# Raw weight pieces ahead of stores and convolution loads, and a new order in the first group, in a two-layer convolution and FFN kernel

## What is computed

```python
# layer 0
h   = grouped_conv1d(x, weight, taps=9, groups=4) + (c @ c_weight.T)[:, :, None] + bias
y   = h @ W.T + bias_k + lora(h)        # W: 1024 x 1024, low-rank part of rank 3 x 16
x   = x + y
# layer 1
att = softmax(mlp(c))                   # 8 experts' weights per batch
h   = (att-weighted 64 x 64 matrix) @ x + (att @ bias_k)[:, :, None]
s   = h @ Wr.T                          # 64 scores per token, the best 16 kept, softmax -> G
z   = ((h @ A) * G) @ B                 # A: 1024 x 1024, B: 1024 x 1024
x   = x + 2 * z
```

## Time and profile before

| | |
|---|---|
| runs | 703.81, 704.87, 707.1 us: median 704.87 |
| the profiled execution | 702.36 us |
| its span | 700.5 us, at a mean granted clock of 0.975 |
| TensorE (PE) | busy 662.5 us (95%) |
| VectorE (DVE) | busy 452.5 us (65%) |
| ScalarE (ACT) | busy 213.0 us (30%) |
| GpSimd (POOL) | busy 77.9 us (11%) |
| DMA | 157.98 MB, mean 226 GB/s |

### The profile page before, as it was taken

One profiled execution on the slowest core, in us unless ns is written; L12 is line 12 of the kernel. 1 busy time (PEld: TensorE's weight loads), 2 busy tenths in 40 slices (PEclk: granted clock), 3 DMA queues, 4 the chain that ended last, 5 costly groups with the idle time before them and its releaser, 6 DMA issues.

```text
span 700.5 us, 8826 instructions
## 1 busy us (share of the span) xinstructions
PE 662.5 (95%) x3197; PEld 546.1 (78%) x3197; DVE 452.5 (65%) x688; ACT 213.0 (30%) x275; POOL 77.9 (11%) x91
## 2 busy tenths in 40 slices
PE   9979999949789999999799999999799999999996
PEld 8858888837578788888589888887588978888875
DVE  2877866628248749626957858645866965756764
ACT  2631434215023412323413411323512521243510
POOL 1599200000000024000000006000000000000000
PEclk9998999979989999999999999999999999999999
DMA  8589744773973771076797664066688566127594
GB/s 286 201 283 390 276 194 139 276 265 115 387 245 122 300 300 61 31 271 221 284 338 253 265 257 157 11 231 226 232 302 308 197 263 274 30 97 214 203 334 177
DMA packets 51449, 157.98 MB, mean 226 GB/s; under 512 B 5472, under 2 KB 6368, under 8 KB 51424
## 3 DMA queue, kind: packets, MB, share of 16 engines
q1 hardware_dynamic: 46096, 148.05, 58.2%
q10 hardware_dynamic: 5328, 9.61, 4.2%
HBM read 131.94 MB, written 25.71 MB: 225 GB/s over the span
## 4 chain that ended last, share of the span: by engine, by line
PE 51%; DMA 7%; DVE 5%; issue 3%; ACT 2%; SPq 1%; ACTq 0%; DVEq 0%
PE bank L1304 13%; PE bank L1306 13%; PE bank L1305 13%; PE bank L1318 6%; DMA raw<-pieces 4%; PE bank L1338 3%; PE bank L1325 2%; DMA gate_x<-gates 1%; DMA piece_lo<-kept 1%; ACT piece_hi L603 1%; DVE piece_lo L846 1%; DVE work L941 1%; PE bank L1344 1%; PE bank L1330 1%; PE bank L1332 1%
## 5 line engine op out<-in xcount | busy, mean ns | idle before, releaser
L846 DVE TENSOR_TENSOR piece_lo<-raw,piece_hi 128x1024 fp32r<-128x1024 f32 x60 | 74.2, 1241 | 101.7 <-ACT piece_hi L603 101.7
L1304 PE MATMUL bank<-piece_hi,u_hi 128*128 128x512 f32 x272 | 113.8, 418 | 25.2 <-DVE piece_lo L996 15.4
L603 ACT ACTIVATE piece_hi<-raw 128x1024 fp32r<-128x1024 f32 x60 | 63.1, 1057 | 160.3 <-PE bank L1306 109.4
L1305 PE MATMUL bank<-piece_lo,u_hi 128*128 128x512 f32 x272 | 111.6, 410 | 0.0
L1306 PE MATMUL bank<-piece_hi,u_lo 128*128 128x512 f32 x272 | 111.2, 409 | 0.0
L1304 PE MATMUL bank<-v_hi,piece_hi 128*128 128x512 f32 x256 | 101.9, 398 | 0.0
L1306 PE MATMUL bank<-v_hi,piece_lo 128*128 128x512 f32 x256 | 101.1, 395 | 0.0
L1305 PE MATMUL bank<-v_lo,piece_hi 128*128 128x512 f32 x256 | 100.9, 394 | 0.0
L1304 PEld LDWEIGHTS bank<-piece_hi,u_hi 128*128 128x128 f32 x272 | 54.1, 199 | 41.9 <-DVE piece_lo L996 16.7
L1304 PE MATMUL bank<-piece_hi,v_hi 128*128 128x512 f32 x192 | 75.9, 396 | 0.7 <-DMA piece_lo<-kept 0.7
L1306 PE MATMUL bank<-piece_hi,v_lo 128*128 128x512 f32 x192 | 75.8, 395 | 0.0
(11 more groups left out here) (141 smaller groups left out, 820.8 us busy)
## 6 DMA issues: line engine op xcount, KB each, us to landing
raw<-pieces SPq DMA_DIRECT2D x84, 512.0 KB, 4.9
piece_hi<-kept SPq DMA_DIRECT2D x48, 512.0 KB, 4.6
piece_lo<-kept SPq DMA_DIRECT2D x48, 512.0 KB, 5.6
conv_in<-conv_x SPq DMA_DIRECT2D x16, 516.0 KB, 6.5
x<-x SPq DMA_DIRECT2D x16, 512.0 KB, 5.1
gate_x<-gates ACTq DMA_DIRECT2D x32, 256.0 KB
out<-x SPq DMA_DIRECT2D x32, 256.0 KB, 2.3
conv_in<-pieces SPq DMA_DIRECT2D x12, 512.0 KB, 7.9
```

What stands on the lines that cost most here:

```text
L603: act.activation(piece_hi[:, n % SLOTS, :], raw[:, r % RAWS, :], ACT.Copy).then_inc(s_piece_hi, 1)
L846: dve.tensor_tensor(piece_lo[:, n % SLOTS, :], raw[:, r % RAWS, :], piece_hi[:, n % SLOTS, :].bitcast(F32), ALU.subtract).then_inc(s_piece ...
L1304: pe.matmul(to, left_hi, right_hi, start=first, stop=False)
L1305: pe.matmul(to, left_hi, right_lo, start=False, stop=False)
```

## The change

On SP, in the first group: `next_raw(8)` goes ahead of the loads and stores of sums; the stores of unit 2 are taken apart in pairs, with raw 16 between them and raw 17 behind them, and the loads of unit 3 follow raw 17 in one block; the stores of unit 3 and the convolution loads are taken in pairs with raw 22 and raw 23 between them. In the loop, each of the four convolution loads follows one of `next_raw(16)` to `(19)`, and the two bias tables follow `next_raw(20)` and `next_raw(21)`.

On ScalarE and VectorE, in the first group: the low-rank mask and factors come ahead of split 5, and VectorE's `combine(0)` is cut in two, with mask and factors between its halves; splits 5 and 6 come ahead of the halves of unit 0's sums; on ScalarE split 11 comes ahead of the copy of the scores and split 13 and two halves of unit 2 ahead of the copy of the gates; split 14 comes ahead of the gate loads; `combine(3)` moves from behind the gated chunks to behind chunk 5, and split 19 to behind chunk 7.

```diff
--- before.py
+++ after.py
@@ -406,12 +406,12 @@
                 sp.wait_ge(s_out_ctx, 16)
                 cond_bias(0)
                 next_raw(7)
+                next_raw(8)
                 for i in range(4):
                     sp.wait_ge(s_comb_in[i], 16)
                     load_weights(1, i)
                 for step in range(4):
                     keep_weights(0, step)
-                next_raw(8)
                 next_raw(9)
                 next_raw(10)
                 for step in range(2):
@@ -424,17 +424,26 @@
                 mix_bias(0)
                 next_raw(14)
                 next_raw(15)
+                keep_weights(2, 0)
+                keep_weights(2, 1)
                 next_raw(16)
-                for step in range(4):
-                    load_weights(3, keep_weights(2, step))
-                for n in range(17, 22):
+                keep_weights(2, 2)
+                keep_weights(2, 3)
+                next_raw(17)
+                for i in range(4):
+                    load_weights(3, i)
+                for n in range(18, 22):
                     next_raw(n)
-                for step in range(4):
-                    keep_weights(3, step)
-                for t in range(NT):
-                    load_conv_in(1, t)
+                keep_weights(3, 0)
+                keep_weights(3, 1)
                 next_raw(22)
+                keep_weights(3, 2)
+                keep_weights(3, 3)
+                load_conv_in(1, 0)
+                load_conv_in(1, 1)
                 next_raw(23)
+                load_conv_in(1, 2)
+                load_conv_in(1, 3)
                 next_raw(24)
                 for t in range(NT):
                     store(0, t, 0, t + 1)
@@ -468,17 +477,18 @@
                 next_raw(15)
                 for n in range(11, 14):
                     fetch(g, n)
-                next_raw(16)
-                next_raw(17)
-                next_raw(18)
-                next_raw(19)
+                for n in range(16, 20):
+                    next_raw(n)
+                    if not last:
+                        load_conv_in(g + 1, n - 16)
+                next_raw(20)
                 if not last:
-                    for t in range(NT):
-                        load_conv_in(g + 1, t)
                     cond_bias(g)
+                next_raw(21)
+                if not last:
                     mix_bias(g)
-                for n in range(20, 24):
-                    next_raw(n)
+                next_raw(22)
+                next_raw(23)
                 next_raw(24)
                 next_raw(25)
                 fetch(g, 26)
@@ -732,14 +742,12 @@
                 split_first(3)
                 split_first(4)
                 biases_out(1, s_mixb, 3, s_out_mixb)
-                split_first(5)
-                for step in range(2):
-                    combined_hi(0, step)
                 mix_bias()
                 lora_parts(0)
-                for step in range(2, 4):
+                split_first(5)
+                split_first(6)
+                for step in range(4):
                     combined_hi(0, step)
-                split_first(6)
                 split_first(7)
                 split_first(8)
                 for step in range(4):
@@ -750,25 +758,28 @@
                     if c % 2 == 0:
                         act.wait_ge(s_comb[c // 2], 32 * 2)
                     split_hi(0, MIX0 + c, v_hi[:, c, :], work[:, c, :])
+                split_first(11)
                 score_out(0, 4)
-                split_first(11)
                 gates_exp(0)
                 split_first(12)
+                split_first(13)
+                combined_hi(2, 0)
+                combined_hi(2, 1)
                 gates_out(0, 6)
-                split_first(13)
+                combined_hi(2, 2)
+                combined_hi(2, 3)
+                split_first(14)
                 act.wait_ge(s_gates_out, 16)
                 for c in range(GATES):
                     spread_gates(c)
-                for step in range(4):
-                    combined_hi(2, step)
-                split_first(14)
                 split_first(15)
                 for c in range(NCH):
                     if c % 2 == 0:
                         act.wait_ge(s_comb[c // 2], 32 * 3)
                     gated_hi(0, c)
-                    if c in (1, 3, 5, 6):
+                    if c in (1, 3, 5):
                         split_first(16 + c // 2)
+                split_first(19)
                 for step in range(4):
                     combined_hi(3, step)
                 for n in range(20, 24):
@@ -996,13 +1007,16 @@
                     dve.tensor_tensor(piece_lo[:, n % SLOTS, :], raw[:, n % RAWS, :],
                                       piece_hi[:, n % SLOTS, :].bitcast(F32), ALU.subtract).then_inc(s_piece_lo, 1)
 
-                def combine(unit):
-
-                    for i in range(4):
-                        dve.wait_ge(s_comb_in[i], 16 * (unit + 1))
+                def combine(unit, part=None):
+
                     b11, b12, b21, b22 = (raw_weights(unit, i) for i in range(4))
-                    dve.tensor_tensor(b11, b12, b11, ALU.subtract).then_inc(s_sum, 1)
-                    dve.tensor_tensor(b12, b22, b12, ALU.subtract).then_inc(s_sum, 1)
+                    if part != 1:
+                        for i in range(4):
+                            dve.wait_ge(s_comb_in[i], 16 * (unit + 1))
+                        dve.tensor_tensor(b11, b12, b11, ALU.subtract).then_inc(s_sum, 1)
+                        dve.tensor_tensor(b12, b22, b12, ALU.subtract).then_inc(s_sum, 1)
+                    if part == 0:
+                        return
                     dve.wait_ge(s_sum, 4 * unit + 2)
                     dve.tensor_tensor(b22, b22, b11, ALU.subtract).then_inc(s_sum, 1)
                     dve.wait_ge(s_sum, 4 * unit + 3)
@@ -1047,13 +1061,14 @@
                 mix_bias()
                 dve.wait_ge(s_adapter, 14)
                 split_first(4)
-                combine(0)
-                split_first(5)
+                combine(0, 0)
                 masked(0, 4)
                 lora_rest(0)
+                combine(0, 1)
+                split_first(5)
+                split_first(6)
                 for step in range(4):
                     combined_lo(0, step)
-                split_first(6)
                 split_first(7)
                 for h in range(2):
                     for t in range(NT):
@@ -1087,9 +1102,11 @@
                 split_first(12)
                 split_first(13)
                 combine(2)
-                for step in range(4):
-                    combined_lo(2, step)
+                combined_lo(2, 0)
+                combined_lo(2, 1)
                 split_first(14)
+                combined_lo(2, 2)
+                combined_lo(2, 3)
                 split_first(15)
                 dve.wait_ge(s_lo, H0)
                 for c in range(NCH):
@@ -1097,9 +1114,11 @@
                     if c % 2 == 0:
                         dve.wait_ge(s_comb[c // 2], 32 * 3)
                     gated_lo(0, c)
-                    if c in (1, 3, 5, 6):
+                    if c in (1, 3, 5):
                         split_first(16 + c // 2)
-                combine(3)
+                    if c == 5:
+                        combine(3)
+                split_first(19)
                 for step in range(4):
                     combined_lo(3, step)
                 for n in range(20, 23):
```

## The result

The median after is 685.71 us (682.83 to 686.93 in four runs) against 705.94 in the four runs beside it: a ratio of 0.9715, with an interval of 0.9679 to 0.9751, or 20.2 us less. The forecast was 670.5 with a range of 663 to 684. The direction was right and the size was not: about two fifths of the expected gain are missing, and the time lies 1.7 us beyond the range.

The account below looks back on a forecast made before the run. TensorE was taken as the bound, busy 95% of the span, gains coming from waits and lowered clock. 702.4 - 23.4 (first group) - 11.3 (loop) + 1.0 (opening, mix) = 668.7; 671.2 by the median, stated 670.5, range 663 to 684.

Parts of the forecast that it names:

- The loop: Middle loop groups: convolution loads behind raw loads bring piece 20 earlier; the whole difference from the last group, 11.3 us, won.
- Rival two: Loop: its gain fails because the gate loads were slow, not piece 20; 682 us, chance 0.10.
- The opening and the mix: First group's start: earlier mask wins 5.3 us, not kept; TensorE waits at mix and score 4 instead; 1.0 us lost.
- The reason given for the late last store: Opening: raw 7 and on leave SP 4.6 us later, behind split 5, so unit 1's last store lands at 94.1 to 96.7.
- the 2.3 us of the estimate: Opening: by the skill's exclusion rule a moved VectorE sum could wait out a GpSimd instruction, 2.3 us; not counted.
- The middle of the first group: Three waits for raw pieces' low halves go with their clock loss: 22.0 us, 23.4 with the loop's first convolution.
- margins of 4 to 5 us: Middle of the first group: least time by which pieces, 19 and 20, would be ready before TensorE needs them.
- rival one: Middle: loads come later because stores and loads share engines, overrunning margins; 6 to 8 us more, 678; chance 0.17.
- The loop's first convolution: Its 1.4 us wait for four additions goes, as splits for the next group end near 183, before TensorE's last product.
- Rival three: Opening: its 5.3 us are kept since unit 1's stores don't land later; 665 us, chance 0.09.
- rival four: Middle: unit 3's sums wait for late loads, delaying gate products; slower from a landing at about 183, 709 up; chance 0.02.
- rival five: Whole kernel: nothing moves, other waits of the same size stand behind those named; 703 to 706 us, chance 0.04.

Follow-up runs that it names:

- e6: The changed kernel with split 5 ahead of the low-rank factors on ScalarE and right behind the mask on VectorE: 682.92 us, ratio 0.9714.
- e3: The changed kernel with gate loads turned to 16 ranks outermost instead of eight rows, A and B laid out to match: 678.9 us, ratio 0.9645.
- e5: The changed kernel with VectorE's four additions ahead of its split of the third piece for group 1: 677.1 us, ratio 0.962.
- e2: The changed kernel with the loop's SP order of before: 697.55 us, ratio 0.9914.
- e10: e7 plus raw 23 straight behind raw 22 on SP: 669.04 us, ratio 0.9507.
- e9: The changed kernel with raw 23 straight behind raw 22 on SP, ahead of the last four stores and the convolution loads: 685.46 us, ratio 0.9742.
- e7: The changed kernel with gate loads 16 outermost, unit 3 sums behind split 19, additions ahead of the third split, split 5 early: 669.43 us, ratio 0.9508.

## Why the prediction was right or wrong

**The loop: right.** Both waits for `u_lo` are gone, and with them the 4.3 us for line 846's low halves, which the prediction left out of its list of waits ("nearly all idle time lies in a few places": of 38.0 us idle the list has 25.2) but had in its 11.3 us, as that was taken from the whole stretch. Piece 20 of group 1 is split at 297.76, 15.7 us after the transposed scores (about 15 was named); the middle groups take 79.32 and 78.82 us (79 to 80 were named), and the loop's part alone gives them 10.1 us. Rival two, that the gate loads were at fault and the order wouldn't help, fell. It had half a point: the gate loads do hold half of the engines, and in the kernel of before they were one of two things late.

**The opening and the mix: right in place, partly by luck in size.** The mask runs at 46.92 (46.65 was named) and TensorE resumes at 49.22 (49.45), after 0.95 us at a clock of 1.00. Raw 7 leaves at 52.97 (53.5), the last store of unit 1 is waited for until 95.08 (94.1 to 96.7), and the transposed scores are 1.0 us later (101.97 before, 103.00 after), just the 1.0 that was taken. The new wait came at the mix items in one piece of 4.2 us, with 1.7 of clock, where two of 2 and 3 were named. That TensorE simply comes early is borne out: VectorE's addition that it waits for starts at 85.93, and before at 85.97. The reason given for the late last store isn't. SP issues the first store of unit 1 at 74.67 before, 74.97 after and 74.44 in e6, whether raw 7 left at 48.91, 52.97 or 48.40. So the start of the raw pieces doesn't set it, and that the scores come just 1.0 us later is luck. VectorE's sums of unit 1, which those stores wait for, start at 65.00, 66.08 and 65.12. By the row of before, VectorE's four low halves beside GpSimd were to stay at 1.15 us each. Here the four take 6.57 us, 1.64 each. Three of them in VectorE's timeline:

```profile
54.42 4.89 DVE L1031 TENSOR_TENSOR v_lo<-work,v_hi 128x1024 fp32r<-128x1024 f32 x3
```

That is some 0.5 us more each, beside a GpSimd busy 4.66 of these 4.89 us. So what the Trainium skill (SBUF — State Buffer, section Who interferes with whom) says of the two engines' exclusion bore on this placing where I went by the row, and the row itself had another side. Before, the low halves kept their 1.15 us and GpSimd's two copies beside them lasted 6.29 us (from 51.61); after, with two of VectorE's sums beside them, the copies last 2.63 us (from 49.23). The moved sums take 1.21 and 1.30 us (1.53 and 1.65 before), so nothing near the 2.3 us of the estimate shows there. What the longer low halves cost the kernel wasn't separated.

**The middle of the first group: wrong in the size of the DMA queue.** The step that failed is "the DMA queue served in order at 1.26 us per load or store: [...] about 17 us of work". First, the count was wrong by its own terms: eight stores, two pieces and four loads are 14 x 1.26 = 17.6 us, and the eight gate loads, half the size, are another 5.0, so 22.7. Second, the price was wrong for the gate loads. Alone they move some 190 GB/s on half of the engines (174 to 199 from 121 to 125 us of before), so 256 KB take about 1.38 us of those eight: 17.6 + 8 x 1.38 = 28.7 us, an estimate from these rows, and 29.9 with raw 18 behind them: 148 instead of the 144 named. It landed at 153. The remaining 5 to 6 us stand in the windows at a full share and low rate (318 GB/s from 120 to 130, 353 in e3, when stores and loads are mixed), and their cause wasn't separated. The e3 run takes 4.7 us off piece 18's landing, where the two prices of the gate loads differ by 8 x (1.38 - 0.63) = 6.0.

As a result pieces 17 and 18 were 6 and 9 us later than worked out. The margins of 4 to 5 us were overrun, and the sums of unit 3 stood in line on top. The cost is 2.1 + 4.5 us of waits and 1.5 of clock, 8.1 us together. Of the signs named, ScalarE's first gated split came at 125.81 (before 125 was named, 134.21 before the change), so the stores it depends on did leave early, and piece 17's split at 142.02 missed its 137. This is rival one in outcome: the loads come later than worked out, waits stand at pieces 18 and 19 (19 and 20 were named), and the price is close (6 to 8 us). Its reason, stores and loads sharing the engines, is at most the unexplained rest; the half-width gate loads were in no rival. It got a chance of 0.17, set beside margins that rested on the wrong sum. The row for it was in sight: 58 to 70 at 417 GB/s was taken for the whole queue, though no gate load is in that stretch.

**The loop's first convolution: wrong.** The step that failed is "The 1.4 us in the loop's first convolution goes too: [...] these splits end near 183". The last of them started at 201.03 and ended at 202.3, 19 us late. Piece 23 was split at 186.65 instead of 174, and from there the chain took 15.6 us to the end of the third split, where 9 were allowed; so even with piece 23 in time it would have ended near 190, after TensorE's last product (186 in the forecast). The chain from piece 19 on passes the delay down, as each raw piece waits for the low half two before it, and between raw 22 and raw 24 lie four stores and four convolution loads. The price is 5.4 us of wait and 2.7 of clock. With the rule of the first group (a late queue means late splits) this was to be foreseen: the additions stand behind the third split in VectorE's order, before and after the change, so they take every delay of the raw pieces. The edit e5 shows it by taking 6.7 to 8.6 us back (3.6 between the two profiled executions). No rival had it. Rival three fell with the opening, rival four needed unit 3's loads to land at 183, where the sums on them began at 155.66, and rival five with the waits that went.

**The sum.** Forecast for the profiled execution 668.7, measured 682.8: 14.1 us. The waits of the middle with their clock are 8.1, the convolution's wait 5.4 and its clock 2.7, together 16.2. Against them the loop gave about 1.3 more than forecast (12.6 for 11.3), and smaller terms the remaining 0.8: 16.2 - 1.3 - 0.8 = 14.1. The two failed steps thus account for the miss. The balance adds waits of one execution, and they aren't independent: in e3 part of what the middle gave came back as a longer wait in the convolution. With four further edits (e3 to e6) the kernel takes 669.4 us, which is near the time that the forecast wanted from the change alone; e3 changes the gate loads themselves, so this agreement doesn't confirm the forecast's sum.

## What to carry to other kernels

When loads are put ahead of stores in a full DMA queue, the wait can merely change its place, as it did here, unless the queue's whole work fits in the time: sum it per DMA engine, not per core, and look at the outermost dimension of each transfer, since one of 8 used half of the engines here. Look also at what stands in an engine's program order between the late step and the one that the bound engine waits for: moving four additions ahead of a split that nobody needed yet was worth 7 to 9 us, the same order as the whole reordering of the first group.

## What the runs showed of the hardware that I had not expected

- Loads with an outermost dimension of 8, alone in flight, kept the DMA share at 0.50 to 0.55, with 174 to 199 GB/s (before, 121 to 125 us); with 16 outermost, the queue around them moved 413 GB/s instead of 371 (130 to 140 us, e3 against after).
- Issuing a DMA took SP longer while the queue was full. Two rows of SP's timeline in the changed kernel:

```profile
118.17 0.43 SPq L389 DMA_DIRECT2D kept<-u_lo  x1
...
125.85 1.50 SPq L388 DMA_DIRECT2D kept<-u_hi  x1
```

  The same instruction lasts 0.43 us at first and 1.1 to 1.85 us from 119.42 on. The eight stores and raw 16 take from 117.80 to 128.99 to be issued, 11.2 us. Raw 17, behind them, had its condition (low half 15) at 125.1. So a piece put behind them isn't only late in the queue, it is late in being issued.
- The granted clock of the 7 us behind a wait, in single executions: 1.00 behind waits of 0.95, 1.54, 2.00, 2.08, 2.30 (e2) and 2.42 us (e10, convolution); lower behind 1.89 (e10, mix, 0.76), 2.42 (e9, 0.78), 2.48 (e7, 0.76), 2.74 (e5, 0.57), 4.20 (0.76), 4.53 (0.79) and 5.38 us (0.62). The two lists overlap (2.42 us stands in both), so the length of the one wait alone doesn't tell. The prediction had "2.7 us or more", from before's rows.
